# A macaron layer on one core: normalization statistics, row maxima and the feed-forwards of the last two iterations moved

## The reference

```python
# x: (32, 256, 128) float32, 16 heads of 8, hidden 512, weights of the ffn are +1 or -1
def ffn(x):                       # k0 (256,512), k1 (512,512), k2 (512,128) boolean
    h = concatenate([x, -x])      # 256
    h = relu(s0 * h @ sign(k0)) * 2
    h = relu(s1 * h @ sign(k1)) * 2
    return s2 * h @ sign(k2)
def attention(x):
    Q, K, V = x @ W.T + b ; P = softmax(Q K^T / sqrt(8)) per head
    return layernorm(P V + x) * gamma + beta
x = x + 0.5 * ffn(layernorm(x))
x = x + attention(layernorm(x))
x = x + 0.5 * ffn(layernorm(x))
```

## Time and profile before

| | |
|---|---|
| runs | 722.7, 723.79 and 725.0 us, median 723.79 |
| profiled execution | 722.4 us, its span 720.6 us |
| busy, share of the span | PE 676.1 us (94%), DVE 620.2 us (86%), ACT 489.3 us (68%), POOL 475.2 us (66%) |
| granted TensorE clock, mean | 0.998 of full speed |

### The profile page before, as it was taken

The page is one execution under the profiler, slowest core; times in us unless marked ns, Lnnn a source line. Parts: engine busy times, 40 slices in busy tenths (PEclk is TensorE's granted clock), DMA queues, the critical chain, the costliest instruction groups (busy, mean ns, idle before and its releaser), DMA issues. The chain is left out here.

```text
span 720.6 us, 18521 instructions
## 1 busy us (share of the span) xinstructions
PE 676.1 (94%) x7183; PEld 314.3 (44%) x7183; DVE 620.2 (86%) x1229; ACT 489.3 (68%) x704; POOL 475.2 (66%) x789
## 2 busy tenths in 40 slices
PE   7888989999999999999999999999999998888887
PEld 3434343444444344444444444444434444343346
DVE  6778898989899898989989898989989898787766
ACT  3436777777777777776777777777777776776643
POOL 5555488687877868696776868786786875254330
PEclk9999999999999999999999999999999999999999
DMA  3112221221212123212321222121212321010000
GB/s 84 48 42 58 56 69 32 67 62 45 68 37 62 46 68 61 67 47 60 56 44 54 60 69 61 45 69 39 61 46 68 46 67 33 30 40 1 17 2 30
DMA packets 72821, 36.38 MB, mean 50 GB/s; under 512 B 47648, under 2 KB 72736, under 8 KB 72736
## 3 DMA queue, kind: packets, MB, share of 16 engines
q1 hardware_dynamic: 71120, 34.49, 19.4%
q10 hardware_dynamic: 1616, 0.72, 0.4%
HBM read 5.05 MB, written 4.19 MB: 13 GB/s over the span
## 5 line engine op out<-in xcount | busy, mean ns | idle before, releaser
L1314 ACT ACTIVATE probs<-ps_t,score_scale 128x1024 f32<-128x1024 f32 x252 | 279.8, 1110 | 110.9 <-PE ps_t L992 108.3
L1666 DVE TENSOR_REDUCE row_max<-ps_s 128x4 f32<-128x1024 f32 x256 | 311.1, 1215 | 16.9 <-PE ps_s L979 16.4
L1538 DVE SCALAR_TENSOR_TENSOR ffn_lo<-ps_z,ffn_hi 128x512 f16<-128x512 f32 x232 | 158.8, 685 | 49.6 <-ACT ffn_hi L1273 46.3
L858 PE MATMUL ps_z<-ffn_hi,w 128*128 128x512 f16 x464 | 177.3, 382 | 3.0 <-DVE ffn_lo L1538 2.9
L859 PE MATMUL ps_z<-ffn_lo,w 128*128 128x512 f16 x464 | 175.9, 379 | 0.0
L1273 ACT ACTIVATE ffn_hi<-ps_z 128x512 f16<-128x512 f32 x232 | 137.3, 592 | 39.6 <-PE ps_z L848 20.8
L1032 PE MATMUL ps_c<-probs,v_cols 128*32 128x256 f32 x2048 | 131.0, 384 | 1.1 <-ACT probs L1314 0.7
L979 PE MATMUL ps_s<-k_rows,q_rows 32*128 32x256 f16 x1024 | 100.2, 273 | 21.8 <-DVE row_max L1666 18.5
L992 PE MATMUL ps_t<-q_rows,k_rows 32*128 32x256 f16 x992 | 97.1, 273 | 0.0
L979 PEld LDWEIGHTS ps_s<-k_rows,q_rows 32*128 32x128 f16 x1024 | 28.9, 92 | 119.3 <-DVE row_max L1666 80.3
L1032 PEld LDWEIGHTS ps_c<-probs,v_cols 128*32 128x32 f32 x2048 | 56.7, 109 | 54.7 <-issue 27.0
(11 more groups left out here) (224 smaller groups left out, 1084.8 us busy)
## 6 DMA issues: line engine op xcount, KB each, us to landing
x<-L_attn_x SPq DMA_DIRECT2D x16, 256.0 KB, 2.9
q_rows<-q_hi SPq DMA_DIRECT2D x32, 128.0 KB, 2.1
k_rows<-k_hi SPq DMA_DIRECT2D x31, 128.0 KB, 2.1
y<-x SPq DMA_DIRECT2D x15, 256.0 KB, 2.2
q_rows<-no_max SPq DMA_DIRECT2D x16, 128.0 KB, 2.1
q_rows<-q_lo SPq DMA_DIRECT2D x16, 128.0 KB, 2.1
k_rows<-k_lo SPq DMA_DIRECT2D x15, 128.0 KB, 2.1
q_rows<-max_rows SPq DMA_DIRECT2D x64, 8.0 KB
```

The costliest lines, as they stand in the source:

```text
L858: pe.matmul(o[:], w, ffn_hi[:, 1 + k, :], start=(k == 0), stop=False)
L1314: a_.activation(probs[n % PROBS][:, j:j + 2, :], o[:], ACT.Exp, scale=score_scale[:, 0:1]).then_inc(s_exp, 1)
L1538: v.scalar_tensor_tensor(out=ffn_lo[:, use, :], in0=z_bank(f, use)[:], scalar=0.0, in1=ffn_hi[:, use, :], op0=ALU.max, op1=ALU.subtract).t ...
L1666: v.tensor_reduce(row_max[hb % 2][:].rearrange("p (a l) e -> p l a e", a=2)[:, j:j + 2, :, g % 2], ps_s[:].rearrange("p l (a k) -> p l a k ...
```

## The change

It moves or replaces these things:

- The second feed-forwards of the last two iterations (`second_ffn(T - 4)` and `second_ffn(T - 3)`) leave FFNS_ON_PE: GpSimd makes their rows, SP transposes them by transfer. `turn_ffn` stands behind `turn_att` and ahead of `place_max(t, par, 0)` on SP. `ffn_deviation` and `ffn_apply` go.
- Their pieces 1 to 15 (piece 0 is empty on this way) are spread over steps 10 to 31, instead of pieces 0 to 15 over steps 4 to 31. In steps 4, 6 and 8 TensorE gets 4, 4 and 3 warming matmuls. Their statistics move by a step.
- In iterations 0, 14 and 15 VectorE takes the row maxima always ahead of the low part or the residual of the same step.
- In the loop the second feed-forward's bn_stats move from steps 2, 2, 3, 3 to 1, 1, 2, 2, its aggregates from step 4 to 5; the next first feed-forward's aggregates from 22 to 20; the attention norm's bn_stats from 20, 20, 28, 28 to 28, 28, 30, 30 and its aggregates from step 30 to step 1 of the next iteration (AT_PREP_CLOSED), for tiles 3 and up.
- V's projection in the head no longer waits for K's low part; ScalarE's copy of V does instead.

```diff
-PACE_ALONE = {4 + piece * 27 // 15: piece for piece in range(PIECES)}
+PACE_ALONE = {10 + (piece - 1) * 21 // 14: piece for piece in range(1, PIECES)}
...
+WARM_ALONE = {4: 4, 6: 4, 8: 3}
...
-AT_STATS_A, AT_STATS_B, AT_STATS_PREP = ((2, 2, 3, 3), 4), ((8, 8, 10, 10), 22), ((20, 20, 28, 28), 30)
+AT_STATS_A, AT_STATS_B, AT_STATS_PREP = ((1, 1, 2, 2), 5), ((8, 8, 10, 10), 20), ((28, 28, 30, 30), None)
+AT_PREP_CLOSED = 1
...
-AT_STATS_A_ALONE = ((0,) * TT, 1)
+AT_STATS_A_ALONE = ((0, 0, 1, 1), 2)
...
-AT_NORM_A_ALONE = 3
...
-        FFNS_ON_PE = (0, second_ffn(T - 4), second_ffn(T - 3))
+        FFNS_ON_PE = (0,)
...  SP
+                if it.pace and it.stats_a:
+                    turn_ffn(it.ffn_a)
                 if it.cur and it.prev:
                     place_max(t, par, 0)
                 if it.first and it.prev:
                     turn_ffn(it.next_b)
-                elif it.stats_a and by_dma(it.ffn_a):
+                elif it.stats_a and not it.pace:
                     turn_ffn(it.ffn_a)
...  GpSimd
                 if alone:
-                    ffn_deviation(it.ffn_a)
+                    ffn_rows_norm(it.ffn_a, x2[par])
...  TensorE
-            def project_v(use):
-                misc_wait(use)
+            def project_v(use, behind_k=False):
+                if behind_k:
+                    pe.wait_ge(m_free, use - 1)
+                    at_least(pe, mt_free, last_max["m"])
+                    uses_done[0] = use + 1
+                else:
+                    misc_wait(use)
...
+                    elif it in tail and s in WARM_ALONE:
+                        pe.wait_ge(z_free, z_before(it.ffn_a) - 1)
+                        warm(WARM_ALONE[s], z_bank(it.ffn_a, 1)[:])
...
-                            project_v(it.misc["V"])
+                            project_v(it.misc["V"], behind_k=not it.prev)
...  ScalarE
                 act.wait_ge(m_full, use + 1)
+                act.wait_ge(m_free, use)
...  VectorE
+                    norm_late = t >= 2 and not it.pace and s == AT_PREP_CLOSED
...
+                    if norm_late:
+                        att_mean_var_wait(t + 1)
...
-                    maxima_first = any(piece in ffn_mid_done(f) for f, _, piece in pieces)
+                    maxima_first = it.pace is not None or any(piece in ffn_mid_done(f) for f, _, piece in pieces)
...
-                    if norm_prep:
+                    if norm_prep or norm_late:
                         mean_var(att_bn, att_mv, TT, a_mv)
...
-                    if it.pace and it.stats_a and s == AT_NORM_A_ALONE:
-                        ffn_apply(it.ffn_a, x2[par])
```

More of the change, by code:

```diff
@@ L661, in ffn_rows_norm @@
                 ffn_rows_finish(f)
-            def ffn_deviation(f):
-                pool.wait_ge(f_mv, f + 1)
-                inverse_deviation(ffn_rs, ffn_ve, ffn_mv, TT, f_rs, rs_steps(f))
             def att_deviation(t):
@@ L1119, in _ @@
                 elif what == "V":
-                    project_v(3)
+                    project_v(3, behind_k=True)
                 ffn_piece(0, s)
@@ L1595, in solo_norm @@
                 scale_rows(ffn_xn, src, solo_mv, solo_rs, SOLO_ROWS[n]).then_inc(q_xn, 1)
[L1597 to L1603, removed]
             def att_apply(t, par):
@@ L1772, in steps @@
                     if it.own_contexts and s == AT_STATS_SOLO[1]:
-                        dve.wait_ge(z_full, z_use(it.ffn_a, 0) + 1)
+                        dve.wait_ge(f_xn, it.ffn_a + 1)
                         solo_norm(SOLO_BEFORE_LAST, x2[1 - par])
```

## The result

The changed kernel takes 720.0 us (median of 6 runs, 718.5 to 720.4) against 723.6 for the kernel before beside it: a ratio of 0.9948, with a 95% interval of 0.993 to 0.9965. By that ratio it is faster by 3.8 us (0.0052 x 723.6; the medians differ by 3.6); 6.9 were forecast, and the median lies in the forecast range, 711.0 to 721.0. The profiled execution took 718.5, with a span of 716.5 against 720.6. The shares of busy time say nothing about it: TensorE 675.9 us instead of 676.1, VectorE 615.9 instead of 620.2, GpSimd 483.1 instead of 475.2.

What follows compares the result with a forecast made beforehand. The prediction took TensorE, interrupted by waits for VectorE, to bound the loop, and the ring of scores and row maximum the last two iterations. Terms -7.4 - 0.7 + 0.2 + 1.0 = -6.9 us gave 716.9, range 711.0 to 721.0.

Steps and rivals of the forecast that it cites:

- The loop, -7.4: Iterations 2 to 13: three TensorE stalls behind VectorE, 0.38, 0.16 and 0.08 us counted start to start, go twelve times.
- (b): Rival on the loop: part of its stalls re-form, 4.6 us gained instead of 7.4, total 719.7; chance 0.14.
- Iteration 0, -0.7: V's projection without the wait gains 0.8 us, row maxima first 0.2, about 0.3 given back; bounds 0 to -1.3.
- Iteration 14, +0.2: TensorE reaches pair 5 sooner, stands for the transfer, has one first-layer block left over; +0.2 us, bounds -2 to +2.
- Iteration 15 and the end, +1.0: Low part in step 27 ahead of solo statistics delays row maximum 15; +1.0 us, bounds -1.5 to +2.5.
- Landed 13.1: Iteration 15: the transposing transfer lands 13.1 us from the iteration's start, after rows at 10.0.
- pair 13 at 31.8: Iteration 15: pair 13 starts 31.8 us into the iteration, against 32.0 before the change.
- The transposing one of 128 KB: Transfers: a transposing 128 KB transfer lands after 3.1 us, a plain one of 128 KB after 2.1.
- (a): Rival: the loop gives 7.4 us and the rest costs about nothing; 716.9, 714.8 to 719; chance 0.50.
- (d): Rival: the last two iterations lose, TensorE standing for transfers and its clock falling to 1.2 GHz; 721.3 us; chance 0.09.
- (e): Rival: the loop's attention norm, 1 us later, makes Q wait for its transfer; slower, 729 us; chance 0.05.
- its own last sentence: Prediction wrong if the loop period stays above 40.8, or the last two iterations differ over 2 us from 37.9 and 37.1.

Runs made afterwards that it cites:

- loop_a: old_tail_mf with only the second feed-forward's loop statistics still moved; the next first feed-forward's aggregates and the attention norm's statistics go back: 711.9 us, ratio .9833.
- loop_prep: old_tail_mf with the second feed-forward's loop statistics back in steps 2, 2, 3, 3 and 4, the other half of the loop's edit kept: 719.6 us, ratio .9937.
- v_waits: The changed kernel with V's projection waiting for K's low part again, in the head and in iteration 0: 723.2 us, ratio 1.0004.
- only15: The changed kernel with iteration 14's feed-forward back on TensorE's transposes and the transfer in iteration 15 only, row maxima first in both: 715.8 us, ratio .9915.
- aggr_step1: The changed kernel with the second feed-forward's statistics of the last two iterations in step 0 and aggregates in step 1: 715.8 us, ratio .9891.
- the two other repairs: In iteration 15, first context norm's statistics in step 10 (not 11), solo statistics in step 26 (not 27); both with aggr_step1 on the changed kernel: 713.2 us.
- solo_26: The changed kernel with the solo statistics of iteration 15 in step 26 instead of 27: 719.4 us, ratio .9949.
- old_tail_mf: The changed kernel with both last feed-forwards back on TensorE's transposes, old steps, no warming, but row maxima still ahead of low parts: 710.6 us, ratio .9829.

## Why the prediction was right and wrong

- **The loop, -7.4: right, -7.8.** The 0.38 and the 0.16 of the start-to-start count are gone in the trace, the period is 0.64 shorter, and loop_a and loop_prep show the second feed-forward's statistics as the cause. Rival (b) didn't happen: nothing re-formed.
- **Iteration 0, -0.7: -0.54; a term was left out.** V is worth 0.76 (forecast 0.8), and the rest of the edit costs 0.2 (forecast 0.1). The same edit in the head's projection brings iteration 0 forward by about 0.9 us (v_waits). The prediction gave the head no term.
- **Iteration 14, +0.2: right, +0.4.** Pair by pair it is close: pair 5 at 10.1 us (forecast 10.0), the landing at 13.4 (13.3), pair 6 at 14.4 (14.4), the rest 23.9 (23.6), and the clock did stay in the profiled execution. What the forecast didn't see is what the +0.4 is made of: 37.87 before held a fall of the clock that cost 0.9 and not 1.4 (36.98 without); row maxima first take 1.2 where the old way is kept (35.80); the transfer, with the new steps and the warming, costs 2.5 (38.26).
- **Iteration 15 and the end, +1.0: the term that was mis-sized, +4.6, beyond its own bound of +2.5.** It is -0.8 for row maxima first (77.12), +3.6 for the transfer as it lands after 3.1 us (80.69, only15), and +1.8 for the landing after 4.5 with the fall of the clock behind it. Three steps failed. "Landed 13.1" was 14.7, by the fetch of instructions; in only15, without it, it was 13.3 and pair 6 came at 14.3 (forecast 14.2). "I expect 2.4 GHz throughout", written of iteration 14, was carried over to iteration 15, where the clock fell. And "pair 13 at 31.8" was 33.6 even in only15 and 35.5 in the changed kernel, since the forecast had no look at GpSimd's queue, where the maxima's cut stands behind the context's norm. Of the 3.6, aggr_step1 gives back 1.1 (aggregates a step too late) and the two other repairs 2.1; 0.3 are left. What was foreseen is there: pairs 13 to 15 take 5.2 us instead of 4.1, with 1.2 more forecast, and moving the solo statistics ahead of the low part gives back 0.6 of it (solo_26).
- **A wrong reading.** "The transposing one of 128 KB" is a transfer of 0.26 MB, twice that (1056 packets in the DMA view), so it isn't compared with a plain one of its size. The kernel before has plain ones of 256 KB, `y<-x`; they land after 2.2 us, and the transposing one's 3.1 is still the longer.
- **The rivals.** What came is the loop of (a) with half of (d), which had a chance of 0.09: TensorE stood for the transfer in both iterations, and its clock fell behind it, in the profiled execution in one of them. (d)'s price of 1.7 us a fall was too high: a fall cost 0.7 to 0.9 in iteration 14, and the 1.8 in iteration 15 holds the late landing too. (e), Q waiting for the attention norm, is refuted by the row at 448.01.
- **The number.** The forecast of 716.9 was 3.1 us too low, and the measured 720.0 lies above the range of (a), 714.8 to 719. It lies in the whole range because that reaches up to (b) and (d); (b) has nearly this time, 719.7, but its mechanism didn't occur. By its own last sentence the prediction was wrong on iteration 15, whose last pair came 4.6 us later where 2 was the limit. With the last term at +4.6 and the start's -0.8 the forecast's other terms give the -4.1 of the span.
- **Not run apart.** The new steps of the feed-forward's pieces and the warming matmuls in steps 4, 6 and 8 went with the transfer in every kernel; how much of its price is theirs stays open.

## What to carry to other kernels

Look on the engine that feeds the bound one for a crowd and a hole: two small instructions ahead of the one that TensorE wanted cost 0.6 us an iteration, and the hole two steps earlier was free. A way through another engine and a transfer takes work off one queue and puts a long chain ahead of all that it feeds; list each queue in which something then stands behind a late arrival (here VectorE's statistics, behind them GpSimd's cut of maxima, behind that TensorE). And run the parts alone: in this change's last two iterations the small reorder was worth 2.0 us, and the transfers with what came with them cost 7.9 (38.26 and 82.53 against 35.79 and 77.12).

## What the runs showed of the hardware

- A fetch of instructions (one packet of 0.02 MB) in the midst of a transposing transfer of 0.26 MB made it land after 4.5 us instead of 3.1, in four kernels of the eight that have this transfer in iteration 15. A small edit is enough for the two not to meet, since both move with it: the fetch started 2.2 us behind the transfer's issue in the changed kernel, 6.1 behind it in aggr_step1, and 1.0 ahead of it in warm_wait.
- The granted clock of the same kernel differs between executions, and the time with it: old_tail_mf took 710.5 to 710.6 us at a mean of 1.000 and 711.9 at 0.998, the changed kernel 718.5 at 0.998 and 720.1 to 720.4 at 0.990. A single profile can hold a fall of 0.9 us that the comparison then books as somebody's gain.
